# A transformer layer pair on eight cores: one logarithm and one exponential per attention segment, and two background steps per unit

## What is computed

```python
x = x + attn_a(layernorm(x))   # causal, 16 heads of 64, rotary embedding, softmax, projection
x = x + ffn(layernorm(x))      # 1024 -> 4096 -> 1024
x = x + attn_b(layernorm(x))   # not causal, q and k rotated and normed to length 1
x = x + ffn(layernorm(x))      # the same weights as the first
```

```python
def weight_quant(w):
    scale = 1.0 / jnp.clip(jnp.mean(jnp.abs(w)), 1e-05)
    return jnp.clip(jnp.round(w * scale), -1, 1) / scale
```

## Time and profile before

| what | us |
|---|---|
| median of 2 runs | 5035.98 (5035.28 to 5036.68) |
| profiled execution | 5041.35 |
| its span, slowest core (core 1) | 5039.8 |
| cores 0 to 3 | 5018.1 to 5039.8, granted clock 0.770 to 0.776 |
| cores 4 to 7 | 5010.6 to 5019.1, granted clock 0.781 to 0.783 |
| units of attention a, first to last finalize | 473.6 to 1246.5 |
| units of attention b, first to last finalize | 3117.9 to 3935.7 |

### The profile page before, as it was taken

One profiled execution on the slowest core, in us unless ns is written; L12 is line 12 of the kernel. 1 busy time (PEld: TensorE's weight loads), 2 busy tenths in 40 slices (PEclk: granted clock), 3 DMA queues, 4 the chain that ended last, 5 costly groups with the idle time before them and its releaser, 6 DMA issues.

```text
span 5039.8 us, 44924 instructions; the slowest of 8 cores (5010.6 to 5039.8 us)
## 1 busy us (share of the span) xinstructions
PE 3014.2 (60%) x11610; PEld 1007.0 (20%) x11610; DVE 1845.3 (37%) x3077; ACT 2097.6 (42%) x2476; POOL 730.2 (14%) x1290
## 2 busy tenths in 40 slices
PE   2885666666032556757546564777777625757655
PEld 1331111111011222222212221111111212222222
DVE  2211332232226564655533331011100365655653
ACT  1233555555001425243224544777777125234250
POOL 0001222222021213122101110000000302122130
PEclk9776676666555778779877777888888857879898
DMA  5114443322220122213230003001100001213223
GB/s 135 32 38 91 124 132 88 81 81 73 93 65 1 57 65 84 84 55 110 64 78 26 26 26 64 16 16 23 21 16 3 2 23 49 92 57 101 72 81 129
DMA packets 321194, 311.28 MB, mean 62 GB/s; under 512 B 213648, under 2 KB 226224, under 8 KB 320944
## 3 DMA queue, kind: packets, MB, share of 16 engines
q1 hardware_dynamic: 316272, 291.62, 20.1%
q0 software_dynamic: 4672, 16.79, 2.0%
HBM read 270.46 MB, written 50.46 MB: 64 GB/s over the span
## 4 chain that ended last, share of the span: by engine, by line
PE 32%; DVE 19%; ACT 18%; issue 11%; POOL 9%; DMA 8%; SPq 2%; DVEq 1%; ACTq 0%; POOLq 0%
PE pb L585 7%; PE pb L378 6%; PE pb L614 5%; ACT expqb L557 4%; PE squad L544 4%; PE squad L1069 3%; ACT qkbfb L397 3%; DMA wq_tmp<-w2T 2%; PE pb L910 2%; ACT expqa L557 2%; POOL cvo_DD L1042 2%; POOL cvo_B L1042 2%; PE pb L661 2%; DVE hqi_DD L1100 2%; DVE hdeq_DD L1001 2%
## 5 line engine op out<-in xcount | busy, mean ns | idle before, releaser
L557 ACT ACTIVATE expqb<-squad,kconst 128x1024 bf16<-128x1024 f32 x512 | 554.0, 1113 | 169.6 <-PE pb L585 132.7
L557 ACT ACTIVATE expqa<-squad,kconst 128x1024 bf16<-128x1024 f32 x320 | 352.3, 1114 | 234.3 <-PE pb L585 187.9
L1069 PE MATMUL squad<-xqfm_B,wbuf_B 128*128 128x512 bf16 x1024 | 285.0, 428 | 148.7 <-DVE hdeq_B L1001 138.7
L1069 PE MATMUL squad<-xqfm_DD,wbuf_DD 128*128 128x512 bf16 x1024 | 279.4, 422 | 157.7 <-DVE hdeq_DD L1001 153.3
L585 PE MATMUL pb<-expqb,vbufb 128*65 128x512 bf16 x1024 | 360.1, 437 | 0.8 <-ACT expqb L557 0.7
L585 PE MATMUL pb<-expqa,vbufa 128*65 128x512 bf16 x640 | 256.4, 491 | 114.5 <-POOL expqa L569 108.0
L910 PE MATMUL pb<-w2buf_B,hsilu_B 128*128 128x512 bf16 x1024 | 277.4, 407 | 47.8 <-DMA w2buf_B<-w2qT_d 28.2
L910 PE MATMUL pb<-w2buf_DD,hsilu_DD 128*128 128x512 bf16 x1024 | 272.2, 397 | 50.9 <-DMA w2buf_DD<-w2qT_d 25.5
L544 PE MATMUL squad<-qbufb,kbufb 64*128 64x512 bf16 x1024 | 224.9, 429 | 114.2 <-ACT expqb L557 68.0
L1023 ACT ACTIVATE cvo_DD<-hdeq_DD,tapb_DD,tapw_DD 128x512 f32<-128x512 f32 x128 | 104.2, 814 | 440.3 <-POOL hdeq_DD L1012 237.1
L1023 ACT ACTIVATE cvo_B<-hdeq_B,tapb_B,tapw_B 128x512 f32<-128x512 f32 x128 | 104.2, 814 | 438.5 <-POOL hdeq_B L1012 235.8
(11 more groups left out here) (225 smaller groups left out, 4695.9 us busy)
## 6 DMA issues: line engine op xcount, KB each, us to landing
wq_tmp<-w1T SPq DMA_DIRECT2D x64, 512.0 KB, 4.5
wq_tmp<-w2T SPq DMA_DIRECT2D x64, 512.0 KB, 3.7
wbuf_B<-w1qT_d SPq DMA_DIRECT2D x128, 256.0 KB, 2.6
w2buf_B<-w2qT_d SPq DMA_DIRECT2D x128, 256.0 KB, 2.8
wbuf_DD<-w1qT_d SPq DMA_DIRECT2D x128, 256.0 KB, 2.6
w2buf_DD<-w2qT_d SPq DMA_DIRECT2D x128, 256.0 KB, 2.8
x<-x SPq DMA_DIRECT2D x16, 512.0 KB, 28.0
w1qT_d<-wq_bf SPq DMA_DIRECT2D x32, 256.0 KB, 2.8
```

The costliest lines, as they stand in the source:

```text
L557: sb.op("act", lambda e, sqh=sqh, eb=eb: e.activation(out=expq[eb][:, 0:1024], in_=squad[:, sqh * 1024:(sqh + 1) * 1024], func=AF.Exp, sca ...
L1069: sb.op("pe", lambda e, jc=jc, dc=dc, bank=bank, tokbase=tokbase: e.matmul(squad[:, bank * 512:bank * 512 + 512], wbuf[jc % 3][:, dc * 128 ...
```

## The change

Two things are changed, both in `emit_attention`.

In `emit_finalize`, the two copies now go to the two halves of one 65x1024 tile `otb`. One logarithm over 1x1024 and one exponential over 1x1024 take the place of two of each over 1x512. Both matmuls L614 then read their half of `recip`. `recip` and `lnden` have one buffer instead of two, and 65 partitions instead of 128.

In the loop over the units, `next(bg, None)` is called twice per unit instead of once. With 320 units, that makes room for 640 steps where 448 are left, so that the background is emitted completely within the first 224 units. The scores, the exponentials of the units, the products with V, the projection, the ffn and what the background itself does stay as they were.

```diff
-            out=otmp[par][0:65, :], in_=pbank[ob][0:65, :]),
-            reads=[("pb", ob)], writes=[("otmp", par)])
+            out=otb[par][0:65, 0:512], in_=pbank[ob][0:65, :]),
+            reads=[("pb", ob)], writes=[("otb", par)])
...
+        sb.op("act", lambda e, par=par: e.activation(
+            out=lnden[64:65, 0:1024], in_=otb[par][64:65, 0:1024], func=AF.Ln),
+            reads=[("otb", par)], writes=[("lnden",)])
+        sb.op("act", lambda e: e.activation(
+            out=recip[64:65, 0:1024], in_=lnden[64:65, 0:1024],
+            func=AF.Exp, scale=C["k"][64:65, 3:4]),
+            reads=[("lnden",), ("k",)], writes=[("recip",)])
         for hi in range(2):
...
-            sb.op("act", lambda e, hi=hi, par=par, osrc=osrc: e.activation(
-                out=lnden[64:65, par * 1024 + hi * 512:par * 1024 + (hi + 1) * 512],
-                in_=osrc[64:65, :], func=AF.Ln),
-                reads=[okey], writes=[("lnden", par)])
-            sb.op("act", lambda e, hi=hi, par=par: e.activation(
-                out=recip[64:65, par * 1024 + hi * 512:par * 1024 + (hi + 1) * 512],
-                in_=lnden[64:65, par * 1024 + hi * 512:par * 1024 + (hi + 1) * 512],
-                func=AF.Exp, scale=C["k"][64:65, 3:4]),
-                reads=[("lnden", par), ("k",)], writes=[("recip", par)])
+            sb.op("pe", lambda e, hi=hi, ob=ob: e.matmul(
                 pbank[ob + hi][0:64, :], C["ones_row"][64:65, 0:64],
-                recip[64:65, par * 1024 + hi * 512:par * 1024 + (hi + 1) * 512],
+                recip[64:65, hi * 512:(hi + 1) * 512],
                 start=True, stop=True),
...
         if cch == nch - 1:
             emit_finalize(si)
         if bg is not None:
             next(bg, None)
+            next(bg, None)
```

More of the change, by code:

```diff
@@ L496, in emit_attention @@
     expq = [sbuf(f"expq{which}_{i}", (128, 1024), BF16, stack=a2) for i in range(2)]
-    otm2 = [sbuf(f"otm2_{which}{j}", (65, 512), F32, stack=a2) for j in range(2)]
     oh2 = [sbuf(f"oh2_{which}{j}", (64, 512), BF16, stack=a2) for j in range(2)]
-    recip = sbuf(f"recip_{which}", (128, 2048), F32, stack=a2)
-    lnden = sbuf(f"lnden_{which}", (128, 2048), F32, stack=a2)
-    otmp = [sbuf(f"otmp_{which}{j}", (65, 512), F32, stack=a2) for j in range(2)]
+    recip = sbuf(f"recip_{which}", (65, 1024), F32, stack=a2)
+    lnden = sbuf(f"lnden_{which}", (65, 1024), F32, stack=a2)
+    otb = [sbuf(f"otb_{which}{j}", (65, 1024), F32, stack=a2) for j in range(2)]
     prtmp = [sbuf(f"prtmp{which}_{i}", (128, 512), F32, stack=a2) for i in range(2)]
@@ L596, in emit_finalize @@
         sb.op("dve", lambda e, ob=ob, par=par: e.tensor_copy(
-            out=otmp[par][0:65, :], in_=pbank[ob][0:65, :]),
-            reads=[("pb", ob)], writes=[("otmp", par)])
+            out=otb[par][0:65, 0:512], in_=pbank[ob][0:65, :]),
+            reads=[("pb", ob)], writes=[("otb", par)])
         sb.op("dve", lambda e, ob=ob, par=par: e.tensor_copy(
-            out=otm2[par][0:65, :], in_=pbank[ob + 1][0:65, :]),
-            reads=[("pb", ob + 1)], writes=[("otm2", par)])
-        for hi in range(2):
-            osrc = otmp[par] if hi == 0 else otm2[par]
-            okey = ("otmp", par) if hi == 0 else ("otm2", par)
-            sb.op("act", lambda e, hi=hi, par=par, osrc=osrc: e.activation(
-                out=lnden[64:65, par * 1024 + hi * 512:par * 1024 + (hi + 1) * 512],
-                in_=osrc[64:65, :], func=AF.Ln),
-                reads=[okey], writes=[("lnden", par)])
-            sb.op("act", lambda e, hi=hi, par=par: e.activation(
-                out=recip[64:65, par * 1024 + hi * 512:par * 1024 + (hi + 1) * 512],
-                in_=lnden[64:65, par * 1024 + hi * 512:par * 1024 + (hi + 1) * 512],
-                func=AF.Exp, scale=C["k"][64:65, 3:4]),
-                reads=[("lnden", par), ("k",)], writes=[("recip", par)])
-            sb.op("pe", lambda e, hi=hi, ob=ob, par=par: e.matmul(
@@ new lines, in emit_finalize @@
+            out=otb[par][0:65, 512:1024], in_=pbank[ob + 1][0:65, :]),
+            reads=[("pb", ob + 1)], writes=[("otb", par)])
+        sb.op("act", lambda e, par=par: e.activation(
[5 more added lines that the diff above has]
+            reads=[("lnden",), ("k",)], writes=[("recip",)])
@@ L615, in emit_finalize @@
+        for hi in range(2):
+            sb.op("pe", lambda e, hi=hi, ob=ob: e.matmul(
                 pbank[ob + hi][0:64, :], C["ones_row"][64:65, 0:64],
-                recip[64:65, par * 1024 + hi * 512:par * 1024 + (hi + 1) * 512],
+                recip[64:65, hi * 512:(hi + 1) * 512],
                 start=True, stop=True),
-                reads=[("ones_row",), ("recip", par)], writes=[("pb", ob + hi)])
+                reads=[("ones_row",), ("recip",)], writes=[("pb", ob + hi)])
         sb.op("dve", lambda e, p=p, g=g, ob=ob, par=par: e.tensor_tensor(
-            out=ofm[p][0:64, g * 512:(g + 1) * 512], in0=otmp[par][0:64, :],
+            out=ofm[p][0:64, g * 512:(g + 1) * 512], in0=otb[par][0:64, 0:512],
@@ L621, in emit_finalize @@
             in1=pbank[ob][0:64, :], op=ALU.mult),
-            reads=[("otmp", par), ("pb", ob)], writes=[("ofm", p)])
+            reads=[("otb", par), ("pb", ob)], writes=[("ofm", p)])
         sb.op("dve", lambda e, ob=ob, par=par: e.tensor_tensor(
-            out=oh2[par][0:64, :], in0=otm2[par][0:64, :], in1=pbank[ob + 1][0:64, :], op=ALU.mult),
-            reads=[("otm2", par), ("pb", ob + 1)], writes=[("oh2", par)])
+            out=oh2[par][0:64, :], in0=otb[par][0:64, 512:1024], in1=pbank[ob + 1][0:64, :], op=ALU.mult),
@@ L626, in emit_finalize @@
+            reads=[("otb", par), ("pb", ob + 1)], writes=[("oh2", par)])
         sb.op("sp", lambda e, p=p, g=g, par=par: e.dma_start(
```

## The result

The changed kernel takes 5145.34 us (median of 11 runs, beside 5034.52 for the kernel before in 10 runs on the same chip). The ratio is 1.0236, with a 95% interval of 1.0208 to 1.0263: slower, by about 111 us on the difference of the medians. The span of its profiled execution is 5139.2 us on core 6, 99 us over the one read before. The two slowest cores differ (core 6 here, core 1 there), so I compare stretches from event to event rather than times from the start.

What follows compares the result with a forecast made beforehand. The prediction took VectorE's serial background round (load, steps, store) to bound attention a. 5041.35 us profiled, + 70 for two steps, - 3 for the merge gave 5108; the run median lies 5.4 lower: 5103 us, range 5035 to 5165.

Steps and rivals of the forecast that it cites:

- What bounds the kernel, and the background at two steps: Attention a: serial load-step-store rounds bind VectorE, so two steps slow 224 units but remove the 209 us hole: +70 us.
- First pass: Attention a, first 64 units: copy-to-copy periods of 10 + 2n us for n units, 187 us from first to seventh copy.
- rival 2: Background loads get slower, 2.7 instead of 2.0 us, plus the clock's loss side: up to 5175 us, chance 0.18.
- Second pass: Attention a, units 64 to 223: slice rounds, 15 finalizes and four fetches sum to 636 us, last copy at 1313.
- rival 3: Finalizes overlap loads in flight, rounds with one take 10.6 instead of 15.3 us: 71 us less, 5030 us, chance 0.15.
- rival 4: The background hides as before and the hole is saved whole: 4822 us, chance 0.05.
- Fetches: Second pass of attention a: four fetches of a pair lengthen the rounds by 3 us each, 12 in all.
- The last 96 units: End of attention a, without background: 31.8 + 2 x 95.4 = 222.6 us, last copy at 1536.
- The projection: After attention a's last copy: 7.3 us for the finalize, then 62 us for all 256 matmuls, ending at 1605.
- The merged logarithm and exponential: Finalizes of both attentions: first matmul 3.9 us after the copy, each gains 0.5 or loses 1.1 us; -3 us in all.
- earlier return to the upper level: After the merged finalize TensorE works without a break sooner, so its upper clock may return earlier: about 0.3 us less per unit.
- the loss side: Merged finalize with matmuls at the lower clock level: second ends 7.5 us after the copy; +35 us in attention b.

Runs made afterwards that it cites:

- `two_steps_only`: The kernel before with two background steps per unit instead of one, the finalize as before: 5124.12 us, ratio 1.0166 to the kernel before.
- `merge_own_halves`: The kernel before with only the merged logarithm and exponential, and a recorder name for each half of `otb`: 5062.17 us, ratio 1.005 to the kernel before.
- `one_step_prefetch`: The kernel before, one step per unit, with second-pass loads two slices ahead and two bf16 result buffers: 4921.51 us, ratio 0.9774.
- `own_names`: The kernel before with only separate recorder names for the halves of the logarithm and reciprocal tiles: 4956.23 us, ratio 0.9842.

## Why the prediction came out as it did

The forecast was 5103 us, +67 by its own sum. Measured were 5145 and +111. The time lies inside the range of 5035 to 5165, but above the forecast's own 5070 to 5140, and just past the 2% that I had given a chance of 0.18. By its steps:

*What bounds the kernel, and the background at two steps.* Right in mechanism and in size. The sum had +70 us; the second step alone added 74 to attention a (`two_steps_only`). From the first copy to the last projection matmul the prediction had 1605 - 473.6 = 1131 us, without the merge; `two_steps_only` took 1127.0 on core 1, and the changed kernel 1141.6. Some terms came out longer and others shorter, so part of the closeness is luck. The parts, in the changed kernel, with core 1 of `two_steps_only` in brackets:

- First pass: 195.4 us from the first to the seventh copy, for 187 (191.0). The reductions came every 2.0 us in the long burst, as taken (ten intervals from 500.49 to 520.60). The load behind a finalize landed 5.1 to 8.0 us after the start of the second product, where I had 5.3 for all. Loads in the long bursts were no slower than 1.9 to 2.1 us each, so rival 2 falls.
- Second pass, from the seventh copy (654.75) to the copy at unit 223 (1317.66): 662.9 us, for 650.5 (654.9). The first steps of the slices lie 647.8 us apart, for 636 (640.4). A slice of w1 without a finalize took 7.7 us including its fetches, one of w2 9.0, and those with a finalize 16.3 and 16.7. With the fetches set aside, that is about 8.5 us for a finalize of the merged kernel, for 7.8, and about 8.0 in `two_steps_only`. The count of 15 and the order of steps were right; no load was in flight over a finalize. So rival 3 falls, and rival 4 with it.
- Fetches: rounds of 10.3 to 12.5 instead of 7.2 to 8.7, about 3 us each as taken.
- The last 96 units: 218.8 us for 222.6 (216.1). The projection: 64.5 us from the last copy, for 69.3 (65.0). It runs at a granted clock of 0.97.

*The merged logarithm and exponential.* This is the step that failed. The sum had -3 us; the merge cost 27 to 28 us in attention b and 11 to 13 in attention a, about 40, which is nearly all of what the forecast missed. Three things were wrong.

First, the chain to the first matmul was 4.2 us (3514.56 to 3518.73) instead of 3.9. I had read the two copies as 1.3 us, and missed that their common name makes the second wait for the first, 0.85 us between starts instead of 0.61.

Second, I split the difference on the clock, where it went one way. The wait for the reciprocals grew from 2.36 to 4.07 us, and both matmuls ran at the lower level in every finalize (no record under 1052 ns, before down to 587). That the longer wait is what brought the level down is likely and not shown by itself: behind waits of about 2.35 us, in attention b of the kernel before, the first matmul began at the upper level in 17 of 32 finalizes, and behind 3.80 us, in `merge_own_halves`, in none. But in attention a all of them ran at the lower level before the change too, behind waits of mostly 2.14 us, so the wait is not all that decides. The hoped-for earlier return to the upper level did not show: from the next scores to the next first copy a segment takes 19.5 us in both kernels. The granted clock of the stretch is 0.81, and was 0.84 (core 1, 3118 to 3936). By the rule on idle gaps of the Trainium skill (TensorE: Matmul & The Clock Gate, "Why this matters for your kernels") the loss side would hold in every finalize, +35 us in attention b. The trace agrees with it: 28 us. But the second matmul began at the upper level in none of the 32 finalizes before as well, behind the shorter waits.

Third, I let only 10 finalizes of attention a count, at a third. All of them got 0.4 us longer. Where VectorE's queue is the limit, a finalize stands between two slices, so its length adds to the round there too (8.5 us for about 8.0).

The argument that ScalarE's saving is off the path fits the runs: the merge saved ScalarE time and the kernel got slower. The same view held the better edit. The wait of the second exponential for the first matmul, which I named as saved by the merge, was worth 1.6% once it was removed without making the first half wait.

*The signs.* Of what was to show in the trace: no idle stretch before the projection, yes. L601 waiting over 300 us, yes (408). The last L754 near 1310, yes (1316.2). Pairs 2 to 4 at 155 to 170 us: 158.4, 164.4 and 175.4. Pairs 6 and 7 at 95: 94.7 and 93.8. The first matmul 3.9 us after the copy: 4.2. Of what would have been wrong, none showed: a segment of attention b moved by 0.9 us, just under the 1 us named.

## What to carry to other kernels

Background work put into an in-order queue cost what its waits cost here, not what its arithmetic costs. Before raising its rate, measure the whole round (load, work, store, next load) and compare the round times the count with the foreground stretch; if it doesn't fit, take the load out of the round first. Merging two short operations saves time only where their engine is the late one; ScalarE wasn't. On a chain that another engine waits for, look at when the first half is ready. Here the better edit was a finer name for the tile, so that the halves stopped waiting for each other. And take the mean over all repetitions of a short chain before you compare: the one finalize shown in detail was 0.5 us shorter than the average.

## What the runs showed of the hardware

A store's landing depended on what stood ahead of it. In the hole before, with no load in flight, the first store of a slice landed 1.7 us after its issue, and both waits and issues took 2.1 us together. With a load issued 0.6 us before it (`one_step_prefetch`), the first store landed after 3.8 to 4.0 us, and the two took 4.2 to 4.4. This row is from the hole before:

```profile
1302.48 2.14 SPq L780 DMA_DIRECT2D w2qT_d<-wq_bf  x2
```

Two matmuls run back to back, with a wait of 4.07 us before them, did not bring the upper clock level back. In the finalize shown above TensorE is busy for 3.64 us in a row, and the scores behind it still ran at the lower level, 0.61 us for the pair against 0.39 in steady units. And the level fell although the second wait was short: in the finalize of `own_names` shown above, the first matmul ran at the upper level (1.04 us) behind 2.35 us of waiting, and the second, 0.38 us behind its end, at the lower one (1.94 us).
